# Row sums on VectorE in place of small products in the opening of a two-part graph network

## The reference

```python
h = jnp.maximum(_layernorm(x, axis=-1), 0.0)
# first attention, with inp = h
h = inp @ W                               # W is 256x256
Wh1 = h @ a[:F_out, :]                    # one number a row: "s"
Wh2 = h @ a[F_out:, :]                    # one number a row: "r"
e = jax.nn.leaky_relu(Wh1 + Wh2.T, ALPHA)
attention = jax.nn.softmax(jnp.where(mask, e, NEG_INF), axis=1)
...
```

## Time and profile before

| | |
|---|---|
| median of 3 runs | 2601.47 us (2601.43 to 2603.41) |
| time of the profiled execution | 2604.16 us |
| span of its trace (first to last instruction) | 2602.4 us |
| mean granted TensorE clock over the span | 0.989 of 2.4 GHz |
| busy, share of the span | TensorE 96%, VectorE 84%, ScalarE 65%, GpSimd 59% |
| the opening, to the start of s_quad | 60.56 us |

### The profile page before, as it was taken

One profiled execution on the slowest core, in us unless ns is written; L12 is line 12 of the kernel. 1 busy time (PEld: TensorE's weight loads), 2 busy tenths in 40 slices (PEclk: granted clock), 3 DMA queues, 4 the chain that ended last, 5 costly groups with the idle time before them and its releaser, 6 DMA issues. The chain is left out here.

```text
span 2602.4 us, 47910 instructions
## 1 busy us (share of the span) xinstructions
PE 2496.5 (96%) x18492; PEld 2363.2 (91%) x18492; DVE 2190.1 (84%) x2917; ACT 1685.2 (65%) x2316; POOL 1523.0 (59%) x932
## 2 busy tenths in 40 slices
PE   7699999999999979999999999987999999999997
PEld 5588888888888869999999999987999999999997
DVE  5899999999999647888888898894788888888888
ACT  5999999999999655555555555553555555555554
POOL 4899999999999702444444444450345444444446
PEclk9799999999999989999999999999999999999999
DMA  3332322232323031333333233233233333333333
GB/s 110 115 94 90 94 90 93 90 93 90 93 90 94 13 104 49 98 94 105 94 101 103 90 106 98 90 114 110 66 94 118 98 101 115 97 103 110 102 99 105
DMA packets 100979, 248.21 MB, mean 95 GB/s; under 512 B 9360, under 2 KB 51088, under 8 KB 100752
## 3 DMA queue, kind: packets, MB, share of 16 engines
q1 hardware_dynamic: 98880, 243.30, 30.5%
q10 hardware_dynamic: 1872, 1.84, 0.2%
HBM read 232.52 MB, written 12.58 MB: 94 GB/s over the span
## 5 line engine op out<-in xcount | busy, mean ns | idle before, releaser
L91 PE MATMUL l0b_acc<-l_h_parts,l0b_turned_hi 128*128 128x512 f32 x1984 | 727.2, 406 | 19.6 <-POOL l0b_turned_lo L579 19.5
L579 POOL TENSOR_TENSOR l0b_turned_lo<-l0b_turned,l0b_turned_hi 128x1024 fp32r<-128x1024 f32 x256 | 614.3, 2415 | 44.7 <-ACT l0b_turned_hi L616 42.8
L92 PE MATMUL l0b_acc<-l_h_parts,l0b_turned_lo 128*128 128x256 f32 x1984 | 558.4, 281 | 0.0
L1171 POOL TENSOR_TENSOR g0b_sum_wide<-g0b_sum_wide,g0b_slab 128x512 f32<-128x512 f32 x240 | 311.2, 1297 | 396.5 <-DVE g0b_masked_psum L1279 386.4
L1171 POOL TENSOR_TENSOR g1b_sum_wide<-g1b_sum_wide,g1b_slab 128x512 f32<-128x512 f32 x240 | 315.5, 1315 | 339.5 <-DVE g1b_masked_psum L1279 328.7
L91 PEld LDWEIGHTS l0b_acc<-l_h_parts,l0b_turned_hi 128*128 128x128 f32 x1984 | 376.1, 190 | 112.8 <-POOL l0b_turned_lo L579 29.7
L92 PEld LDWEIGHTS l0b_acc<-l_h_parts,l0b_turned_lo 128*128 128x128 f32 x1984 | 374.2, 189 | 0.9
L616 ACT CAST l0b_turned_hi<-l0b_turned 128x1024 fp32r<-128x1024 f32 x256 | 268.1, 1047 | 67.4 <-PE l0b_acc L92 50.3
L80 PE MATMUL g0b_acc<-g_wh_parts,g0b_part_hi 128*128 128x256 f32 x1024 | 293.6, 287 | 6.8 <-DVE g0b_part_lo L1285 5.7
L80 PE MATMUL g1b_acc<-g_wh_parts,g1b_part_hi 128*128 128x256 f32 x1024 | 293.6, 287 | 5.6 <-DVE g1b_part_lo L1285 4.5
L80 PE MATMUL g0b_score_psum<-g0b_q_block,g_vt_hi 128*128 128x256 f32 x1024 | 290.3, 284 | 2.5 <-DVE g0b_q_block L1315 1.4
(11 more groups left out here) (234 smaller groups left out, 7221.2 us busy)
## 6 DMA issues: line engine op xcount, KB each, us to landing
g_adj_ring<-in_adj_blocks_dram SPq DMA_DIRECT2D x256, 512.0 KB, 3.6
l_adj_ring<-in_adj_quads_dram SPq DMA_DIRECT2D x128, 512.0 KB, 3.6
l0b_x_in<-in_x_dram SPq DMA_DIRECT2D x32, 128.0 KB, 2.4
x_rows<-l0b_x SPq DMA_DIRECT2D x32, 128.0 KB, 2.3
g0a_rows<-x_rows SPq DMA_DIRECT2D x8, 512.0 KB, 5.4
g0b_y<-x_rows SPq DMA_DIRECT2D x16, 256.0 KB, 4.0
v_rows<-g0b_y SPq DMA_DIRECT2D x16, 256.0 KB, 4.5
g1a_rows<-v_rows SPq DMA_DIRECT2D x8, 512.0 KB, 5.0
```

The costliest lines, as they stand in the source:

```text
L91: pe.matmul(out, lhs_hi, rhs, start=first, stop=False)
L92: return pe.matmul(out[:, width:], lhs_lo, rhs[:, :width], start=False, stop=False)
L579: pool.tensor_tensor(turned_lo[:, m % PART_RING, :, :], turned[:, m % TURN_RING, :, :], turned_hi[:, m % PART_RING, :, :].bitcast(F32), AL ...
L1171: pool.tensor_tensor(sum_wide[:], sum_wide[:], half_of(c, e), ALU.add).then_inc(summed, 1)
```

## The change

s is no longer made by TensorE. u_s is made as a vector repeated on all partitions (a_wide gets two more columns of a, and u_s comes from two products of 256 columns), stays in PSUM, and VectorE makes s of a tile as one multiply of the normalised tile by it, with the sum along the row as its accumulator output (take_s). Each sum waits for the one before (s_made). The copies of u_s and of the s columns go. The statistics of part 3, the last, move ahead of the copy of group 2, and the sums are put behind take_r of the same group.

```diff
-            a_wide = mem.sbuf("a_wide", [P, KT, P])
-            u_s = mem.sbuf("u_s", [P, KT])
+            a_wide = mem.sbuf("a_wide", [P, 2 * KT, P])
+            junk = mem.sbuf("junk", [P, D])
...
-            s_psum, s_rows = u_psum[:, 0:4 * T], u_psum[:, 4 * T:5 * T]
-            u_s_psum, u_r_psum = u_psum[:, 0:KT], u_psum[:, D:2 * D]
+            u_s_psum, u_r_psum = u_psum[:, 0:D], u_psum[:, D:2 * D]
+            s_psum = u_r_psum[:, 0:4 * T]
...
+                    def take_s(g):
+                        for t in range(g * TURNS, (g + 1) * TURNS):
+                            dve.wait_ge(norm.normed, t + 1)
+                            wait(dve, s_made, t)
+                            dve.scalar_tensor_tensor(out=junk[:], in0=rows[:, t, :], scalar=1.0, in1=u_s_psum,
+                                                     op0=ALU.mult, op1=ALU.mult, accum_out=s_high[:, t:t + 1]
+                                                     ).then_inc(s_made, 1)
...
-                    for k in range(KT):
-                        dve.tensor_scalar(a_wide[:, k, :], ones[:], a_in[:, KT + k:KT + k + 1],
+                    for k in range(2 * KT):
+                        dve.tensor_scalar(a_wide[:, k, :], ones[:], a_in[:, k:k + 1],
...
-                    dve.tensor_copy(u_s[:], u_s_psum).then_inc(u_copied, 1)
                     dve.tensor_copy(u_r[:], u_r_psum.rearrange("p (k n) -> p k n", n=P)).then_inc(u_copied, 1)
                     copy_turned(0)
                     take_statistics(2)
                     norm.affine(dve, parts[2], 2)
                     copy_turned(1)
-                    copy_turned(2)
-                    take_r(0)
                     take_statistics(3)
                     norm.affine(dve, parts[3], 3)
-                    for g in range(3, GROUPS):
+                    for g in range(2, GROUPS):
                         copy_turned(g)
                         take_r(g - 2)
+                        take_s(g - 2)
                     take_r(GROUPS - 2)
+                    take_s(GROUPS - 2)
+                    take_s(GROUPS - 1)
                     take_r(GROUPS - 1)
-                    dve.wait_ge(s_ready, 1)
-                    dve.tensor_copy(s_high[:], s_rows).then_inc(s_made, 1)
...
-                    pe.wait_ge(a_spread, KT)
-                    for m in range(KT):
-                        for k in range(KT):
-                            pe.matmul(u_s_psum[:, m:m + 1], w_turned[:, k * D + m * P:k * D + (m + 1) * P],
-                                      a_in[:, k:k + 1], start=(k == 0), stop=(k == KT - 1))
+                    pe.wait_ge(a_spread, 2 * KT)
+                    for k in range(KT):
+                        pe.matmul(u_s_psum, a_wide[:, k, :], w_turned[:, k * D:(k + 1) * D],
+                                  start=(k == 0), stop=(k == KT - 1))
...
-                        for i in range(TURNS):
-                            t = g * TURNS + i
-                            for k in range(KT):
-                                last = pe.matmul(s_rows[:, t:t + 1], h_turned[:, g % 2, k, i * P:(i + 1) * P],
-                                                 u_s[:, k:k + 1], start=(k == 0), stop=(k == KT - 1))
...
-                    pe.wait_ge(s_made, 2)
+                    pe.wait_ge(s_made, T + 1)
```

More of the change, by code:

```diff
@@ L263, in first_block @@
             s_made = mem.sem("s_made")
-            s_ready = mem.sem("s_ready")
             s_spread = mem.sem("s_spread")
@@ L410, in _ @@
                                              w_turned[:, k * D + m * P:k * D + (m + 1) * P],
-                                             a_wide[:, k, :], start=(k == 0), stop=(k == KT - 1))
+                                             a_wide[:, KT + k, :], start=(k == 0), stop=(k == KT - 1))
                     last.then_inc(u_ready, 1)
@@ L427, in r_of_group @@
                             pe.wait_ge(h_copied[k], g + 1)
-                        for i in range(TURNS):
-                            t = g * TURNS + i
-                            for k in range(KT):
-                                last = pe.matmul(s_rows[:, t:t + 1], h_turned[:, g % 2, k, i * P:(i + 1) * P],
-                                                 u_s[:, k:k + 1], start=(k == 0), stop=(k == KT - 1))
-                        if g == GROUPS - 1:
-                            last.then_inc(s_ready, 1)
                         wait(pe, r_copied, g - 1)
@@ L441, in _ @@
                     turn_group(0)
-                    pe.wait_ge(u_copied, 2)
+                    pe.wait_ge(u_copied, 1)
                     for g in range(1, GROUPS):
```

## The result

The changed kernel takes 2607.48 us in the median (16 runs, 2605.76 to 2608.3), the kernel before, beside it on the same chip, 2602.21 (16 runs, 2601.31 to 2604.58). The ratio is 1.0018, with a 95% interval of 1.001 to 1.0025: slower by 2.6 to 6.5 us. The forecast was 2601.8, its range ended at 2606.2. The profiled execution has a time of 2607.04 and a span of 2605.3 us. The sixteen runs of the kernel before lie in two groups, nine from 2601.3 to 2602.3 us and seven from 2603.1 to 2604.6; the execution whose profile the prediction read (2604.16) has a time of the upper group.

A forecast was written before the change was run, and what follows sets the result against it. TensorE was taken to bound the opening, VectorE after the change: from 29.9, 28.3 us of copies, take_r and sums plus 0.68 put the spreading product at 58.9, not 58.62; +0.3 on median 2601.47 gave 2601.8 us, range 2599.7 to 2606.2.

The forecast's parts named there:

- What bounds: In the opening (l0a block), TensorE bounds the kernel before at 4.38 us a group; VectorE becomes the new bound.
- Now it is 58.62. The sum is +0.3 us: At the opening's end, the spreading product moves from 58.62 to 58.9 us; 0.3 us is added to the median.
- the early clock: In the opening's first half, TensorE at 1.2 GHz: r takes 3.55 us, a group's transposes 1.92.
- The sums: On VectorE in the opening, 32 added row sums at 0.47 us each, 15.0 us in all.
- the high one (0.54): High bound for each VectorE row sum: accumulator read only after the main part, then the gap, 0.54 us.
- Copy 2: VectorE's copy of group 2's turned rows in the opening begins at 29.9 us, after waiting for the square root of statistics 3.
- its terms (2600.2 and another 1.0 off): Low end of the total: sums at 0.42 us give 2600.2; a root that doesn't hold takes another 1.0 us off.
- signs of being wrong: In the profile after: sums' pitch over 0.6 us, r at 3.55 us past 40, or copy 2 much before 29 or after 31.
- one cancels the other: In the opening, VectorE's shorter group, 3.69 against TensorE's 4.38 us, offsets its start with two copies done at 29.9.
- TensorE staying at 1.2 GHz: Rival: TensorE's clock stays at half through the opening's second half; spreading product at 62.6, +4.0, 2605.5 us; chance 12%.
- Sums at half pace: Rival: each VectorE row sum takes 0.27 us more, 8.6 for 32; +8.9, 2610.4 us; chance 8%.
- The fast case: Rival: VectorE's sums at 0.335 us and no root wait; spreading product at 53.6, -5.0, 2596.5 us; chance 5%.

The follow-up runs named there:

- The four profiles: Four profiled executions of the unedited kernel before, the one the prediction read and three more; spreading product started at 55.1, 56.6, 57.4 and 58.6 us.
- no_sums: Changed kernel with the row sums left out and s set to zero once; median 2597.02 us, ratio 0.9974 to the kernel before, spreading product at 51.07.
- the repeat: The changed kernel measured once more with no edit; median 2606.61 us beside 2603.37 for the kernel before, ratio 1.0014, spreading product at 60.36.
- move_only: Kernel before, s still on TensorE, with only the statistics of part 3 moved ahead of the copy of group 2; median 2608.31 us beside 2601.99, ratio 1.0025.
- order_back: Changed kernel with the statistics of part 3 put back behind the copy of group 2; median 2606.28 us, ratio 1.0011 to the kernel before, spreading product at 59.52.
- free_sums: Changed kernel with four junk buffers, so a sum no longer waits for the one before; median 2603.2 us, ratio 0.9997 to the kernel before.
- order_back_free: Changed kernel with unchained sums and the statistics of part 3 back behind the copy of group 2; median 2601.62 us beside 2602.84 for the kernel before, ratio 0.9998.
- the try to hold its clock: Kernel before with eighteen added identity products on TensorE before 17 us; ratio 0.9999 to the kernel before, spreading product at 56.63, r of group 0 still 3.76 us.

## Why the prediction was wrong

**What bounds, right.** TensorE bound the opening before, and VectorE bounds it now without a pause behind copy 2. A shift of the spreading product passed on, to within what the stretch behind it varies by (2543.5 to 2546.2 us in nineteen profiles).

**The step that failed: "Now it is 58.62. The sum is +0.3 us", put on the median.** The sum compared its 58.9 with the end of one profile and added the difference to a median over runs with other ends. The prediction had the sign in hand: r at 3.55 and transposes at 1.92 us in the first half, 1.80 and 0.88 in the second. It knew them as 1.2 GHz, called them the price of "the early clock", and asked when the clock would rise in the changed kernel alone. In the kernel before they lie on the path of a TensorE-bound opening, and the clock took another course there in each execution. The profile's own time was 2.7 us over the median, which the prediction noted and did not use. The four profiles put the base at 56.9 instead of 58.62: 1.7 us of the miss, give or take 0.7. That it was the latest of four was bad luck; to take one execution for the kernel was not. The same four show what the change gives away: before, early work at 2.4 GHz shortens the opening; after, VectorE bounds, and the two profiles end at 60.35 and 60.36 at two courses of the clock.

**Terms that were mis-sized.** The end came at 60.35, not 58.9.
- The sums: 0.47 forecast, 0.533 chained and 0.343 ahead of another instruction. Of the bounds it was nearly the high one (0.54), the read after the main part and then the gap. 25 x 0.533 + 7 x 0.343 = 15.7 us, not 15.0: +0.7. The rest of VectorE's queue was right: 60.35 - 30.60 = 29.75 us is 15.7 and the 14.0 forecast for six copies, eight take_r and the step to the product.
- Copy 2 at 30.60, not 29.9: +0.7, as late as the load of a made the first affine (9.48 for 8.74). The root stood behind ScalarE's two groups, as forecast, and VectorE waited 1.3 us for it (forecast 1.0). In no_sums, with the same instructions up to copy 2, the first affine came 0.87 us earlier than in the changed kernel, and so did copy 2 (29.73 for 30.60):

```profile
8.61 0.18 DVE L143 RECIPROCAL l0a_norm_scale<-l0a_norm_var 128x4 f32<-128x4 f32 x1 [0.69 <-DMA l0a_a_in<-in_L_gnn_a_dram]
...
29.73 0.68 DVE L339 COPY l0a_h_turned<-l0a_turn_psum 128x512 f32<-128x512 f32 x1
```

So 1.7 + 0.7 + 0.7 + 0.3 (the forecast itself) = 3.4, and 60.35 - 56.9 = 3.5 us. The ratios give 4.7 in the first comparison and 3.6 in the repeat; 3.5 lies inside both intervals. Against the 2601.8 of the forecast the median is 5.7 us late. Of that, 0.7 is the median of the kernel before, 2601.47 in three runs and 2602.21 in sixteen, and 3.1 are the three terms. The rest, nearly 2 us, stays open: the medians of the repeat differ by 3.2 us and not by 5.3, and the stretch behind the opening varies by up to 2.7 us from profile to profile.

The range had a slip of its own: its terms (2600.2 and another 1.0 off) reach down to 2599.2, not 2599.7. And none of the signs of being wrong that the prediction named came: the sums' pitch was 0.53, r took 1.88 to 1.96 us past 40, and copy 2 came at 30.60. All of them looked at the profile after; what failed most was the reading of the profile before.

**The move.** That "one cancels the other" left, against that profile, no more than the two mis-sized terms (58.9 forecast, 60.35 measured), and it hid what the move is worth by itself: 6 us in the kernel before (move_only). Freed of s, TensorE has the slack for it, and undoing it gives 0.8 us (order_back).

**The rivals.** TensorE staying at 1.2 GHz: it ran r 2 at 3.75 us as that rival said, then rose (r took 1.88 to 1.96 us later), and VectorE did not wait. Sums at half pace: no, 0.42 us. The Trainium skill, Vector Engine (DVE) Microarchitecture Reference, section Points that are easy to get wrong, speaks of two sources in SBUF, and the trace agrees that with one in PSUM nothing was lost: 0.42 us, as without accumulator. The fast case (53.6) needed the chain gone and copy 2 early: with the chain gone free_sums ended at 56.5, and with the old order too order_back_free at 54.6.

## What to carry to other kernels

Before a forecast of a few us is put on a median, ask whether the profiled execution is typical of it: its own time beside the median, and equal instructions of unequal duration on the engine that bounds. Work taken from an engine whose clock varies and given to one that it then waits for also gives away the executions in which the clock was good. This rests on the four profiles of one kernel; the try to hold its clock failed. An accumulating instruction that waits for the one before it pays for the read and the semaphore each time; a few output buffers free it. And of a moved step, price first the part that others wait for: eight statistics moved free; the wait for their root, with the fall of the clock in it, cost 6 us.

## What was not expected of the hardware

- The chain of accumulating sums: 0.533 us from start to start, 0.343 without the wait, at the same 0.42 us an instruction. The ELU's chained step without accumulator took 0.46.
- TensorE's clock took different courses in executions of one kernel: the opening of the kernel before ended at 55.1 to 58.6 us, and from the transposes of group 1 to r of group 1 the same instructions, without a pause between them, took 12.37 or 8.67 us.
- The load of a let the first affine start at 8.61 (no_sums) to 9.67 us (order_back) in kernels that issue it alike. It was 8.65 to 9.10 in all seven profiles with u_s as before, and 9.43 to 9.67 in nine of the ten with u_s as changed and a's load behind W's. So the 0.7 us may belong to the change, though no edit touches the load and no run here shows how.
